# Products with the values in runs of up to four chunks, in the multi-query attention loops of a four-part transformer kernel

## What is computed

```python
q = (xn @ Wq).reshape(b, n, H, DH).transpose(0, 2, 1, 3) * scale
k, v = (kv[..., :DH], kv[..., DH:])
k = jnp.concatenate([nk, k], axis=1)
v = jnp.concatenate([nv, v], axis=1)
sim = jnp.einsum('bhid,bjd->bhij', q, k) + bias
sim = jnp.where(causal_mask, neg, sim)
attn = jax.nn.softmax(sim, axis=-1)
out = jnp.einsum('bhij,bjd->bhid', attn, v)
```

## Time and profile before

| | |
|---|---|
| median of 3 runs | 3226.88 us (3223.44 to 3228.7) |
| profiled execution, first to last instruction | 3218.2 us |
| its own time beside that span | not among the three runs; the span lies 8.7 us under their median |
| PE busy | 2924.2 us, 91% |
| DVE, ACT busy | 1882.8 us (59%), 1578.7 us (49%) |
| mean granted TensorE clock | 0.953 of full |
| score rows on DVE (L2438) | first loop from 747.0 us, second 1561.4 to 2007.6, third to 2741.1 |

### The profile page before, as it was taken

One profiled execution on the slowest core, in us unless ns is written; L12 is line 12 of the kernel. 1 busy time (PEld: TensorE's weight loads), 2 busy tenths in 40 slices (PEclk: granted clock), 3 DMA queues, 4 the chain that ended last, 5 costly groups with the idle time before them and its releaser, 6 DMA issues. The chain is left out here.

```text
span 3218.2 us, 50056 instructions
## 1 busy us (share of the span) xinstructions
PE 2924.2 (91%) x17179; PEld 2052.1 (64%) x17181; DVE 1882.8 (59%) x4554; ACT 1578.7 (49%) x3849; POOL 382.5 (12%) x729
## 2 busy tenths in 40 slices
PE   7978999899999998758799999998999999959996
PEld 5746666546777777344577777764667777836664
DVE  5456555346777766777577777345667777332223
ACT  4403555426666661644466666233566666213331
POOL 4560000001111100000000000000111111012222
PEclk8998999999999999879899999998999999979998
DMA  4452221245444321005432321006544443341112
GB/s 123 121 171 64 44 55 28 76 158 162 124 146 145 121 88 39 1 20 160 130 86 68 86 68 35 20 10 195 171 138 126 150 125 104 118 159 34 34 35 92
DMA packets 242482, 308.23 MB, mean 96 GB/s; under 512 B 27261, under 2 KB 185085, under 8 KB 242096
## 3 DMA queue, kind: packets, MB, share of 16 engines
q1 hardware_dynamic: 235082, 285.50, 29.1%
q0 software_dynamic: 7152, 19.54, 2.1%
HBM read 231.31 MB, written 73.21 MB: 95 GB/s over the span
## 5 line engine op out<-in xcount | busy, mean ns | idle before, releaser
L2407 ACT ACTIVATE cond_p<-cond_p,cond_negm 128x128 f32<-128x128 f32 (+7 forms) x768 | 593.2, 775 | 408.4 <-DVE cond_negm L2438 407.5
L2388 PE MATMUL ps_o<-cond_pt,cond_v 128*64 128x256 f32 (+1 forms) x3840 | 478.2, 370 | 5.1 <-DVE attn_out L2474 0.5
L2368 PE MATMUL ps_s<-cond_k_high,cond_q_high 128*128 128x512 f32 (+5 forms) x1152 | 439.4, 387 | 16.8 <-DVE cond_negm L2438 8.3
L2438 DVE CUSTOM_DVE_ANT_0 cond_p<-ps_s,cond_side,cond_null_scores 128x128 f32<-128x128 f32 (+7 forms) x512 | 403.7, 811 | 28.1 <-PE ps_s L2369 22.6
L2369 PE MATMUL ps_s<-cond_k_both,cond_q_both 128*128 128x512 f32 (+5 forms) x1152 | 394.1, 344 | 0.0
L2378 PE MATMUL ps_t<-ident,cond_p 128*128 128x128 f32 x2304 | 348.8, 281 | 6.8 <-ACT cond_pt L2412 4.8
L2388 PEld LDWEIGHTS ps_o<-cond_pt,cond_v 128*64 128x64 f32 x3840 | 237.4, 136 | 180.4 <-issue 89.8
L2378 PEld LDWEIGHTS ps_t<-ident,cond_p 128*128 128x128 f32 x2304 | 250.0, 140 | 106.0 <-issue 77.1
L1507 ACT ACTIVATE attn_pt<-ps_t 128x512 f32<-128x512 f32 (+3 forms) x384 | 173.0, 490 | 237.9 <-PE ps_t L1468 174.6
L2368 PEld LDWEIGHTS ps_s<-cond_k_high,cond_q_high 128*128 128x128 f32 x1152 | 219.9, 191 | 40.1 <-DVE cond_negm L2438 22.3
L2446 DVE COPY cond_pt<-ps_t 128x512 f32<-128x512 f32 (+1 forms) x240 | 140.4, 585 | 166.3 <-PE ps_t L2378 164.6
(11 more groups left out here) (503 smaller groups left out, 4682.1 us busy)
## 6 DMA issues: line engine op xcount, KB each, us to landing
mqa_q_halves<-cond_q_cut SPq DMA_DIRECT2D x96, 512.0 KB, 4.7
cond_q_both<-mqa_q_halves SPq DMA_DIRECT2D x384, 128.0 KB, 3.2
cond_q_high<-mqa_q_halves SPq DMA_DIRECT2D x192, 128.0 KB, 3.0
cond_side<-in_fside_16xSxS SPq DMA_DIRECT2D x32, 512.0 KB, 7.2
moe_experts<-in_L_ffn_W SPq DMA_DIRECT2D x16, 1024.0 KB, 12.2
cond_side<-in_fside_16xSxS SPq DMA_DIRECT2D x32, 448.0 KB, 5.6
cond_side<-in_fside_16xSxS SPq DMA_DIRECT2D x32, 384.0 KB, 5.0
cond_side<-in_fside_16xSxS SPq DMA_DIRECT2D x32, 320.0 KB, 4.6
```

Source lines behind the costliest of these rows:

```text
L2368: nc.tensor.matmul(out, c32(a.Q1[i][:, h, s * P:(s + 1) * P]), c32(a.K1[:, keys]), start=True, stop=False)
L2388: last = nc.tensor.matmul(sums[u % ON][h * HD:(h + 1) * HD, s0 * P:2 * P], a.V[:, b * QB + kb, :], PT[c % PT_SLOTS][:, (2 * h + s0) * P:(h ...
L2407: nc.scalar.activation(p, p, ACT.Exp, bias=negm[u % SMALL][:, r:r + 1], scale=-1.0, accum_out=rsum[u % SMALL][:, r:r + 1]).then_inc(exped, 1)
L2438: nc.vector.tensor_tensor_reduce(out=probs(u, r, 0, q + 1), in0=m.S[k % 2][:, row_offset(L):row_offset(L) + L], in1=toep_back(u, h, L) if ...
```

## The change

In `mqa_order` the two attends per group are replaced. Chunks gather in `waiting`; when there are four, or when the unit's last chunk has been turned (`g == q0`), they all move to `ripe`, and the next group attends to all of `ripe`. A run then holds up to four chunks of one unit: 2 chunks for `q0` = 0, 4 for 2, 4 and 2 for 4, 4 and 4 for 6. Some groups get no attend at all. There are still three slots, six `cond_pt` tiles and the same instructions; lines below L1669 stand three lines further down.

```diff
--- before.py
+++ after.py
@@ -1625,7 +1625,7 @@
 
     places, need = mqa_ring()
     rows = [(u, r) for u in range(len(MQA_UNITS)) for r in range(4)]
-    steps, spreads, waiting = [], [], []
+    steps, spreads, waiting, ripe = [], [], [], []
     ahead, finished, chunk, n_groups = 0, -1, 0, 0
 
     def place(limit, most):
@@ -1665,11 +1665,14 @@
             place(ROWS_AHEAD, 2)
             if spreads and n_groups - spreads[0][0] >= 2:
                 steps.append(("spread", spreads.pop(0)[1]))
-            while len(waiting) > 4:
-                attend(waiting.pop(0))
+            for c in ripe:
+                attend(c)
+            ripe = []
+            if len(waiting) == 4 or g == q0:
+                ripe, waiting = waiting, []
             place(ROWS_AHEAD, len(rows))
             n_groups += 1
-    for c in waiting:
+    for c in ripe:
         attend(c)
     return steps
```

## The result

The changed kernel takes 3322.0 us (median of 4 runs, 3318.7 to 3324.5), the kernel before beside it 3227.8 (4 runs): a ratio of 1.0297, 95% interval 1.028 to 1.0314. It is 94 us slower. The forecast was 3319 us, 92 us slower, in a range of 3290 to 3347.

What follows compares the result with a forecast made beforehand. PE was taken to bound the kernel, busy 28.28 of 28.39 us a period. From the median 3226.9 us, 54 us gained and 146 us lost give net +92, 3319 us, range 3290 to 3347.

Steps and rivals of the forecast that it cites:

- The gain: On PE, 62 fewer runs of attends a loop at 0.29 us each: 1.13 us a period, 54 us gained.
- in front of unit 26's turn: PE's transposes of unit 26 would wait about 0.45 us for the slot of unit 24's spread, until ACT copies it.
- the third short row: PE would wait about 2.2 us at unit 28's third short row, until DVE has read the first from its PSUM bank.
- The loss: DVE's `out` and ACT's spread copy on an alternating chain make PE wait 3.05 us a period, 146 us lost.
- the chain: DVE row, ACT exp, ACT spread copy, DVE `out`, next copy and row, without overlap, followed for units 24 to 28.
- unit 23's `out`: On DVE, it now stands ahead of the chunk copy opening the stretch, adding 0.1 to 0.2 us a period.
- the rival of half the loss: PE held only at the short rows, as DVE begins 1.4 us earlier: 1.6 us a period, +23, 3250 us; 5%.
- POOL's order is unchanged: POOL keeps its order of work under the change; no separate time was added for it.
- DMAs queue nothing new: SP's loads of queries and sides keep their order, shift with the loop, and nothing new waits for them.
- more loss in the bias loops: In two loops, a late spread through POOL's widened inverse costs 1 us for each of 32 periods, 3351 us; 7%.
- The rule on strict FIFOs: ACT and DVE are strict FIFOs; if DVE could pass its waiting `out`, only the gain would be left.
- The signs named in advance: Second loop's period 30.3 us, four-chunk run about 1.7, `out` idle towards 150, PE busy time down some 50 us.

Runs made afterwards that it cites:

- run 3: Kernel before with one merge of attends in each period of ten groups, 142 runs of attends a loop instead of 158: 3211.5 us, 0.9967.
- run 5: Changed kernel with only DVE's `out` of units of two or four chunks moved one group later: 3230.2 us, 1.0027.
- run 1: Changed kernel with each unit's spread made one group after its first group instead of two: 3312.7 us, 1.0298.
- run 4: Kernel before with a table of attends per group (126 runs of attends a loop) and the spread a group early for `q0` = 0 and 4: 3189.5 us, 0.9901.
- run 6: Kernel before with POOL's masking of the bias tiles one unit later: 3201.0 us, 0.9935.
- run 2: Kernel before, runs of two chunks kept, with each unit's spread made three groups after its first group instead of two: 3263.0 us, 1.0125.
- runs 1 and 7: Run 1, and the same edit on the changed kernel together with POOL's masking one unit later: 3242.6 us, 1.0068 for the latter.

## Why the prediction was right, step by step

- **The gain (predicted 1.13 us a period, 54 in all): right.** The price of a run was measured alone at 0.30 us (run 3) against 0.29 from rows. The same comes out of the changed kernel. Its waits, start to start, are 0.78 in front of unit 26's turn (0.98 from 1797.14 to 1798.12, less the 0.20 of a 448-column matmul), 2.48 at the third short row (2.60 less 0.12) and 0.12 at the fourth. That is 3.38, the period grew by 2.23, and 1.15 is left as the gain.
- **The loss (predicted 3.05 a period): right in place and kind, 0.33 too small.** Two readings were off. First, the links of the chain took 10.22 us from DVE's row at 1795.18 to the first short row, 10.09 in my walk: I let every instruction start 0.03 to 0.05 us after what it waited for, but behind ACT it is more. ACT's spread copy ends at 1797.98 (1797.63 and 0.35), DVE's `out` starts at 1798.08, PE's turn at 1798.12; the rows of before already had 0.11 for that `out` (1750.28 and 0.35, then 1750.74). Second, where it begins: that row starts 2.34 us after the unit's first turn, not 2.06 as before. I had added 0.1 to 0.2 for unit 23's `out`, which now stands ahead of it. The trace gives another reason:

```profile
1793.44 0.42 DVE L2477 TENSOR_TENSOR attn_out<-ps_o,cond_rs 128x256 f32<-128x256 f32 x1
1793.78 0.15 DVE L2455 TENSOR_TENSOR cond_nulla<-cond_negm,cond_null_scores 128x4 f32<-128x4 f32 x1
1793.97 0.69 DVE L2449 COPY cond_pt<-ps_t 128x512 f32<-128x512 f32 x1
1794.89 0.16 DVE L2463 TENSOR_TENSOR cond_dn<-cond_rsum,cond_nulle 128x4 f32<-128x4 f32 x1 [0.23 <-ACT cond_nulle L2419]
```

  The copy behind that `out` stands as far behind the turn as before (1.13 us). It is `den` that waits, for ACT's `null` behind an exp, which is late because DVE's row ahead of it (1792.40) starts 0.44 us ahead of the turn, for 0.90 before. That row had waited in turn for ACT's `null` of unit 24 and for PE's scores, which now come directly ahead of the turns, without attends between them. So the late start goes back to PE's new order and not to that `out`, as far as the trace shows; no run moves it alone. The wait in front of unit 26's turn was 0.78 for my 0.45 by both readings: 0.28 from the start, 0.14 from ACT's copy to PE.
- **"DVE begins the stretch 1.4 us earlier" (the rival of half the loss): the other way round.** It began 0.28 later.
- **Why the total still fits: three errors that partly cancel, so the closeness of 3319 to 3322 is luck.** 48 periods times 2.23 is 107 us, 15 more than forecast. A second term I had at nothing: the clock. Three periods of each loop take 32.1 to 33.6 us for 30.6. One of them, in the second loop:

```profile
1942.74:1976.11 33.37, 30.44 (x210) 23.37 (x208) 20.77 (x58) 20.03 (x50) 1.60 (x4) 0.90 0.27 80
1960.00:1963.10 3.10, 3.10 (x13) 2.64 (x11) 1.69 (x7) 1.91 (x6) 0.00 (x0) 0.50 1.01 305
```

In PE's timeline of it:

```profile
1958.92 0.47 PE L2371 MATMUL ps_s<-cond_k_high,cond_q_high 128*128 128x128 f32 x1 [2.31 <-DVE cond_negm L2441]
...
1963.27 2.87 PE L2391 MATMUL ps_o<-cond_pt,cond_v 128*64 128x256 f32 x16
```

  The granted clock is 0.50 (1.2 GHz) from the wait at the short rows on, and the run of four full chunks takes 2.87 us, for 1.95 at full clock (the same run at 1808.32). The three periods cost about 6 us a loop, 18 in all. In the kernel before and in run 5, where PE's waits are shorter or absent, no period of the loops behind the first has a reduced clock. Third, the other way: PE's wait for POOL's inverse, which made the bias loops of the kernel before longer by 7.6 and 10.8 us, is gone:

```profile
L2400 PE MATMUL ps_t<-ident,cond_rb 128*128 128x128 f32 x288 | 57.7, 282 | 0.0
```

  What hides it was not isolated. Together: 16 times 2.23 and 6 is 42 us for the second loop, less 7.6 and 10.8 in the others 34 and 31. From first score row on PE to last `out` they grew by 40.6, 34.0 and 30.7: 105.3 us, where the profiled spans differ by 102.3 and the medians of the runs by 94.
- **"POOL's order is unchanged", and DMAs queue nothing new: true, but incomplete.** The rival "more loss in the bias loops" had the sign wrong: in this kernel the POOL wait got cheaper, not dearer. It was right about the mechanism, which struck in run 1, where the spread came earlier.
- **The rule on strict FIFOs.** A `[1.64 <-ACT cond_rs L2425]` in front of ready work is what such a queue does (the Trainium skill, TensorE: Matmul & The Clock Gate, the part on the array's architecture), and run 5 prices it: moving the waiting instruction behind the ready ones gave back some 87 us, 48 times 1.72 (83 us) by the periods and the reduced clock on top, less what differs outside them.
- **The signs named in advance** came: 30.62 us a period (30.3 said), 1.74 us for a run of four chunks (about 1.7), `out` idle 157 us (towards 150). PE's busy time fell by 18 us and not by 50. In a steady period it fell by 0.60 us and not by 1.13: the matmul ahead of each wait counts with its whole recorded length (0.28 us at 1803.20, where the next one otherwise starts 0.12 later), so 0.16 us of each wait reads as busy. And the periods with a reduced clock have more of it (30.44 us for 27.68). The busy sum is a poor meter of such a gain.

What stays open: the 0.78 us at the slot that holds the spread was never removed alone, nor was the 0.86 that run 5 leaves at the short rows. That the reduced clock follows from PE's waits is read from which runs have it; no run changes the clock alone. Deferring the `out` of every unit would need a second place for the sums, in the free half of the same PSUM bank, written by PE while DVE reads the other half; that wasn't tried. The Trainium skill (PSUM — Partial Sum Buffer, PSUM bank collisions raise a hardware error) says that two engines may not access one bank within the same quadrant of 32 partitions at once, different columns included; no run here shows it.

## What to carry to other kernels

When a group of work is moved in an order that several in-order engines share, follow the small instruction at its end (here a 0.42 us `out`), not the matmuls: what it waits for, and what now stands behind it. Price a gain by one minimal edit (one merge a period), and put the merges where no consumer is pulled ahead of its producer; that turned a 3% loss into a 1% gain (run 4). An engine that looks idle (POOL, 12% busy) can hold up PE through one operation that waits for a DMA: keep such an operation as late in its queue as its reader allows.

## What the runs showed that I had not expected

In the kernel before, POOL's masking wait cost 20 us (0.65%, run 6), where the groups of instructions put 15.2 us on it. The same wait cost nothing with the spread a group later (run 2) and some 70 us with the spread a group earlier (runs 1 and 7), of which PE's waits for POOL are 52.6 and the rest goes with the reduced clock after them: a wait on an engine with 88% idle time is free or dear by the place of one 0.40 us copy behind it. The changed kernel pays for its own waits in the same way, some 18 us at half clock that none of my sums had.
